# Cross-attention kernel: the layer norm of x moved from TensorE's transposes to a transposed load, a subtraction in place and a scale on the scores

## The chip, the cores and the metric

The kernel runs on one core of a Trainium2 chip. The metric is device time in microseconds (us) of one execution; a lower time is better. Five units work side by side and wait for each other through semaphores: TensorE (PE, matrix products and transposes), VectorE (DVE), ScalarE (ACT), GpSimd (POOL), and SyncE (SP), which here only issues transfers (DMAs). ACT issues a few DMAs too, on a queue of its own.

## The reference

x is (8, 128, 512), ctx is (8, 128, 512); there are 8 groups of 4 heads with 128 numbers each (H = 32 query heads, 8 key/value heads).

```
xn = layernorm(x)                       # (x - mean) / sqrt(var + 1e-5), over the 512
q, k, v = xn @ Wq, ctx @ Wk, ctx @ Wv   # Wq 512x4096, Wk and Wv 512x1024
q, k = rope(q), rope(k)                 # cos and sin rows gathered by position
scores = q k^T / sqrt(128), masked; attn = softmax(scores)
x = x + (attn v) @ Wo
x = x + ffn(layernorm(x))               # router, softmax, top 8, mix of 64 rows
```

The mean and the variance of a row of x are the same for all 512 columns of that row, and so (xn @ Wq) is ((x - mean) @ Wq) / sqrt(var + eps).

## The kernel before, in words

All matrix products run in two-part precision: each f32 operand is split into a rounded part (`hi`, by ACT) and a rest (`lo`, by DVE or POOL), and a product is three matmuls. The queries use Strassen's scheme with seven products (`m1` to `m7`) on half-size blocks. For that x is needed transposed (columns on partitions), as four blocks B11, B21, B12, B22 and four sums of them, T1 to T4; all lie in `x_raw`, and each is split into `x_hi` and `x_lo`.

The order of the work is written out by hand, engine by engine. The start of the program, up to about 125 us of the profiled execution, is the part that the change touches:

- SP issues the loads of ctx, Wv, x, Wk, the mask and the first query weights (`load_pair`), and between them the stores of the values (`store_v`, 16 pieces). SP's DMAs are served in the order of issue.
- PE computes 16 pieces of the values (lines 1824 to 1832 and 1847 to 1864), each into one of four PSUM banks; a bank is free again when DVE (pieces 0 to 9) or ACT (10 to 15, `copy_values`) has copied it to `v_stage`. A slot of `v_stage` is free when its store has landed (`dma_vout`). Between the pieces PE turns the gathered cos and sin rows (line 1810), and, after pieces 8 to 11, the normalised x (`transpose_x`, line 1844): 8 rows of the batch, four transposes of 128x128 each.
- DVE takes the statistics of x (lines 1318 to 1324), POOL raises var + eps to the power -0.5 (line 605), DVE normalises each batch row (`normalise_x`, line 1293), PE turns it, ACT copies it to `x_raw` (`copy_x`, line 918).
- POOL then builds the sums of the first query weights (`sums12`, `sum3`, `sum4`, line 554), two of their rests (`lo_w`, line 587), the x sums of the first batch half (`sum_x(0)`, lines 616 to 621), two more rests, and `sum_x(1)`. ACT rounds x (`hi_x`, line 928), DVE takes the rests (`lo_x`, line 1309), and between them both split Wk (`hi_wk` line 912, `lo_wk` line 1298). A third Wk tile can be loaded only when `lo_wk` has freed a slot of the two in `ring_a`.
- Then come 16 key products (lines 1866 to 1873, four banks again), each followed by a rotation: ACT swaps halves (lines 826, 827), POOL multiplies by sin (line 543), DVE by cos and adds (lines 1252, 1257). The first queries follow, and from about 140 us a loop over 64 steps (group, batch row) in which scores, softmax, values and output of one step overlap with the next group's queries. In each step DVE scales and masks the scores (line 1407, one instruction, the scale 128^-0.5 as a constant), ACT takes the exponentials (line 1005).

Of the kernel before, what the change touches and what calls it, by code (L numbers as in the profile page):

```python
# [18 lines left out]
F32 = mybir.dt.float32  # L19
# [45 lines left out]
X_AFTER = 8  # L65
X_ORDER = 0, 4, 1, 5, 2, 6, 3, 7
# [15 lines left out]
def xattn_ffn(nc, x, ctx, pos, mask, rope, wq, wk, wv, wo, router, router_bias, expert_bias, out):  # L82
    v_dram = nc.dram_tensor("v_dram", (KV * NH * P, HB * D), F32, kind="Internal").ap()
    k_dram = nc.dram_tensor("k_dram", (KV * P, T), F32, kind="Internal").ap()
    with ExitStack() as stack:
# [20 lines left out]
        kT = at("kT", [T], F32, 82)  # L106
        hold = at("hold", [5, W], F32, 86)
# [84 lines left out]
        x_rstd = at("x_rstd", [B], F32, 206.90625)  # L192
# [28 lines left out]
        x_bank = [probT, attnT]  # L221
# [28 lines left out]
        rstd_done = sem("rstd_done")  # L250
        norm_done = sem("norm_done")
# [6 lines left out]
        x_ps = sem("x_ps")  # L258
        x_copied = sem("x_copied")
# [137 lines left out]
        def _(sp):  # L397
# [35 lines left out]

            v_tiles = v_dram.rearrange("(g n p) (b d) -> n b p g d", g=KV, n=NH, d=D)
# [45 lines left out]
            sp.wait_ge(x_ps, B)  # L480
# [57 lines left out]
        def _(pool):  # L538
# [66 lines left out]
            pool.tensor_tensor(x_rstd[:, :], x_var[:, :], power[:, :], ALU.pow).then_inc(rstd_done, 1)  # L605
# [18 lines left out]
            pool.wait_ge(mask_done, 1)  # L624
            sum_x(0)
# [194 lines left out]
        def _(act):  # L820
# [93 lines left out]
            def copy_x(j):  # L914
                act.wait_ge(x_ps, j + 1)
                b = X_ORDER[j]
                half, rows = b // HB, slice(b % HB * S, (b % HB + 1) * S)
                act.activation(x_raw[:, 2 * half:2 * half + 2, :, rows],
                               x_bank[j % 2][:, :].rearrange("p (a c k) -> p a c k", a=2, c=HALVES), ACT.Copy).then_inc(x_copied, 1)

            def hi_x(i, q):

                cols = slice(q * 2 * S, (q + 1) * 2 * S)
                if i in (B11, B21, B22):
                    act.wait_ge(x_copied, (q + 1) * HB)
                else:
                    act.wait_ge(x_summed, 4 * (q + 1))
# [35 lines left out]
            copy_x(6)  # L963
            copy_x(7)
# [284 lines left out]
        def _(dve):  # L1249
# [62 lines left out]
            for i in range(V_ACT):  # L1312
                copy_values(i)
                if i in (3, 5):
                    half = 0 if i == 3 else 1
                    dve.wait_ge(dma_x[half], 16)
                    for b in range(half * HB, (half + 1) * HB):
                        dve.bn_stats(x_stats[:, b, :], resid[:, b, :]).then_inc(x_counted, 1)
                if i == 5:
                    dve.wait_ge(x_counted, B)  # L1320
                    for b in range(B):
                        dve.bn_aggr(x_mv[:, b, :], x_stats[:, b, :]).then_inc(x_averaged, 1)
                    dve.wait_ge(x_averaged, B)
                    dve.tensor_scalar(x_var[:, :], x_mv[:, :, 1], EPS, None, ALU.add).then_inc(var_done, 1)
# [3 lines left out]
                if i == X_AFTER - 1:  # L1328
                    dve.wait_ge(rstd_done, 1)
                    dve.wait_ge(b_lo, KB * C)  # L1330
                if i >= X_AFTER - 1:
                    normalise_x(2 * (i - X_AFTER + 1))
                    normalise_x(2 * (i - X_AFTER + 1) + 1)
            lo_wk(0)
            normalise_x(6)
            normalise_x(7)
# [109 lines left out]
            stored(0)  # L1446
            make_c11(0, 0)
# [295 lines left out]
        def _(pe):  # L1743
# [93 lines left out]
            def transpose_x(j):  # L1837
                pe.wait_ge(norm_done, j + 1)
                if j == 0:
                    pe.wait_ge(table_done, 2 * NH)  # L1840
                if j >= 2:
                    pe.wait_ge(x_copied, j - 1)
                for c in range(C):
                    last = pe.transpose(x_bank[j % 2][:, c * P:(c + 1) * P], x_norm[:, j % 2, c * P:(c + 1) * P], ident[:, :])
# [375 lines left out]
```

## Time and profile before

| what | value |
|---|---|
| time, median of 3 runs | 585.05 us (585.02 to 585.27) |
| the profiled execution: its time, its span | 585.23 us, 583.2 us |
| granted TensorE clock | 1.000 over the whole span |
| PE, DVE, ACT, POOL busy | 99%, 81%, 70%, 74% |
| chain that ended last, by engine | PE 92%, DVE 3%, issue 2%, ACT 2%, POOL 1% |
| DMA | 44.85 MB, mean 77 GB/s |

The span runs from the first to the last instruction. A busy share is a mean over stages with different limits: PE is busy nearly always, and the chain of waits (the work that ended last, followed backwards) runs through PE for 92% of the span. In the first 15 slices of 14.6 us the DMA engines are busy for most of the first two and little after. A granted clock of 1.000 means 2.4 GHz.

### The profile page before, as it was taken

What the parts mean: (1) busy time and instruction counts of PE and PEld (TensorE: products, weight loads), DVE (VectorE), ACT (ScalarE), POOL (GpSimd) and SP (SyncE); (2) the same over time, 40 slices, a digit from 0 to 9 for tenths busy, and PEclk for the clock granted to TensorE, in tenths of its full rate; (3) what the DMA queues carried; (4) which work ended last, traced back from release to release, by engine and by line L of the source; (5) the groups of instructions that cost most, each with busy time, mean ns of one, the idle gap of its engine ahead of it and who ended that gap; (6) DMA issues with size and microseconds to landing.
All of it is one profiled execution on the core that took longest, in us unless ns stands there. A gap on an engine that the chain in (4) does not pass through costs nothing.

```text
span 583.2 us, 10605 instructions
## 1 busy us (share of the span) xinstructions
PE 576.2 (99%) x2991; PEld 488.6 (84%) x2991; DVE 471.7 (81%) x764; ACT 406.3 (70%) x1078; POOL 430.8 (74%) x404
## 2 busy tenths in 40 slices
PE   9999999999999999999999999999999999999997
PEld 7788888877888888888888888888888888888885
DVE  5779797699797779877987798779877986797986
ACT  6377654797777767767776777777776776586655
POOL 5577699698986878688868886788678865446554
PEclk9999999999999999999999999999999999999999
DMA  8953526113301310131113110211122011100012
GB/s 278 367 166 97 169 90 216 38 37 103 97 19 56 91 55 20 54 90 54 32 40 90 54 54 20 88 54 54 36 72 69 3 57 54 36 20 0 19 38 90
DMA packets 30831, 44.85 MB, mean 77 GB/s; under 512 B 3024, under 2 KB 11600, under 8 KB 30800
## 3 DMA queue, kind: packets, MB, share of 16 engines
q1 hardware_dynamic: 30112, 43.56, 23.7%
q0 software_dynamic: 256, 0.52, 0.2%
q10 hardware_dynamic: 432, 0.40, 0.2%
q8 instruction: 14, 0.23, 0.2%
q14 instruction: 17, 0.14, 0.1%
HBM read 34.51 MB, written 9.96 MB: 76 GB/s over the span
## 4 chain that ended last, share of the span: by engine, by line
PE 92%; DVE 3%; issue 2%; ACT 2%; POOL 1%; DVEq 0%; ACTq 0%
PE score L1885 9%; PE outp L1909 9%; PE outp L1913 9%; PE outp L1917 8%; PE bank_a L1760 5%; PE bank_a L1762 5%; PE bank_a L1761 5%; PE probT L1964 4%; PE attnT L1746 2%; PE attnT L1747 2%; PE attnT L1748 2%; PE bank_c L1762 2%; PE bank_c L1760 2%; PE bank_c L1761 2%; PE bank_a L1746 1%
## 5 line engine op out<-in xcount | busy, mean ns | idle before, releaser
L543 POOL TENSOR_TENSOR rot<-rot,sinT 128x512 f32<-128x512 f32 x75 | 102.9, 1372 | 45.1 <-ACT rot L827 45.0
L1005 ACT ACTIVATE probs<-score,negmax 128x128 f32<-128x128 f32 x256 | 90.5, 366 | 28.6 <-DVE negmax L1415 28.6
L661 POOL TENSOR_TENSOR probs<-probs,rsum 128x512 f32<-128x512 f32 x62 | 67.1, 1083 | 44.2 <-DVE rsum L1421 44.2
L1909 PE MATMUL outp<-wo_hi,oT_hi 128*128 128x512 f32 x240 | 95.0, 398 | 0.2 <-DVE wo_lo L1482 0.2
L1913 PE MATMUL outp<-wo_lo,oT_hi 128*128 128x512 f32 x240 | 93.5, 391 | 0.3 <-POOL wo_lo L548 0.3
L1917 PE MATMUL outp<-wo_hi,oT_lo 128*128 128x512 f32 x240 | 83.4, 390 | 0.0
L1428 DVE TENSOR_TENSOR resid<-resid,outp 128x512 f32<-128x512 f32 x60 | 41.0, 684 | 48.8 <-PE outp L1917 46.9
L1885 PEld LDWEIGHTS score<-kT,qT 128*128 128x128 f32 x512 | 66.9, 191 | 4.9
L1257 DVE TENSOR_TENSOR qT<-qT,rot 128x512 f32<-128x512 f32 x57 | 68.5, 1205 | 2.9 <-POOL rot L543 0.5
L1132 ACT ACTIVATE oT_hi<-attnT 128x512 fp32r<-128x512 f32 x64 | 38.0, 594 | 43.1 <-PE attnT L1748 41.9
L1014 ACT ACTIVATE pT_hi<-probT 128x512 fp32r<-128x512 f32 x64 | 38.4, 599 | 42.5 <-PE probT L1964 41.9
L1885 PE MATMUL score<-kT,qT 128*128 128x128 f32 x512 | 67.4, 274 | 0.0
L1440 DVE TENSOR_TENSOR oT_lo<-attnT,oT_hi 128x512 fp32r<-128x512 f32 x64 | 44.2, 690 | 14.4 <-ACT oT_hi L1132 14.3
L548 POOL TENSOR_TENSOR wo_lo<-ring_b,wo_hi 128x512 fp32r<-128x512 f32 x30 | 38.6, 1318 | 21.6 <-ACT wo_hi L885 21.6
L1909 PEld LDWEIGHTS outp<-wo_hi,oT_hi 128*128 128x128 f32 x240 | 45.0, 188 | 10.3 <-DVE wo_lo L1482 1.1
L1917 PEld LDWEIGHTS outp<-wo_hi,oT_lo 128*128 128x128 f32 x240 | 45.1, 188 | 10.1
L1913 PEld LDWEIGHTS outp<-wo_lo,oT_hi 128*128 128x128 f32 x240 | 45.1, 188 | 9.9 <-POOL wo_lo L548 0.7
L1005 ACT ACTIVATION_READ_ACCUMULATOR probs<-score,negmax 128x1 f32 x256 | 52.0, 203 | 0.0
L1760 PE MATMUL bank_a<-x_hi,w_hi 128*128 128x512 f32 x120 | 51.9, 433 | 0.0
L1407 DVE SCALAR_TENSOR_TENSOR score<-score,mask_bias 128x512 f32<-128x512 f32 x64 | 44.5, 695 | 6.3 <-PE score L1885 3.0
L1762 PE MATMUL bank_a<-x_hi,w_lo 128*128 128x512 f32 x120 | 47.4, 395 | 0.0
L1761 PE MATMUL bank_a<-x_lo,w_hi 128*128 128x512 f32 x120 | 47.0, 391 | 0.0
(361 smaller groups left out, 1532.0 us busy)
## 6 DMA issues: line engine op xcount, KB each, us to landing
ring_b<-in_wo SPq DMA_DIRECT2D x32, 256.0 KB, 2.9
ring_a<-in_wq SPq DMA_DIRECT2D x28, 256.0 KB, 2.8
v_dram<-v_stage SPq DMA_DIRECT2D x16, 256.0 KB, 4.5
v_raw<-v_dram SPq DMA_DIRECT2D x16, 256.0 KB, 2.6
k_dram<-k_stage SPq DMA_DIRECT2D x14, 256.0 KB, 2.1
kT<-k_dram SPq DMA_DIRECT2D x14, 256.0 KB, 2.9
ctx_in<-in_ctx SPq DMA_DIRECT2D x8, 256.0 KB, 6.8
ring_b<-in_wv SPq DMA_DIRECT2D x8, 256.0 KB, 7.7
```

Of the source, the lines that this page charges most:

```text
L543: pool.tensor_tensor(rot_of(k0), rot_of(k0), sinT[:, half * W:(half + 1) * W], ALU.mult).then_inc(sin_done, 1)
L661: pool.tensor_tensor(probs[:, p], probs[:, p], rsum[:, p, :].unsqueeze(2).broadcast_to([P, GH, S]), ALU.mult).then_inc(soft_done, 1)
L1005: last = act.activation(probs[:, p, h, :], heads(score[p][:, :])[:, h, :], ACT.Exp, bias=negmax[:, p, h:h + 1], accum_out=sums[:, p, h:h + 1])
L1257: dve.tensor_tensor(dst, src, rot_of(k), ALU.add).then_inc(rope_done, 1)
L1407: dve.scalar_tensor_tensor(heads(score[p][:, :]), heads(score[p][:, :]), SCALE, mask_bias[:, b, :].unsqueeze(1).broadcast_to([P, GH, S]), ...
L1760: pe.matmul(ps[:, :], w[0], m[0], start=start and c == 0, stop=False, skip_group_check=True)
L1761: pe.matmul(ps[:, :], w[0], m[1], start=False, stop=False, skip_group_check=True)
L1762: last = pe.matmul(ps[:, :], w[1], m[0], start=False, stop=stop and c == HALVES - 1, skip_group_check=True)
L1885: last = pe.matmul(score[p][:, h * S:(h + 1) * S], qT[:, half, h, b % HB * S:(b % HB + 1) * S], kT[:, b * S:(b + 1) * S], start=True, stop ...
L1909: pe.matmul(ps[:, :], oT_hi[:, cols], wo_hi[:, h, :], start=h == 0, stop=False)
L1913: return pe.matmul(ps[:, :], oT_hi[:, cols], wo_lo[:, h, :], start=False, stop=stop)
L1917: return pe.matmul(ps[:, :], oT_lo[:, cols], wo_hi[:, h, :], start=False, stop=stop)
```

## The change

x is also handed over transposed (`xt`, 512 x 1024) and loaded from there straight into the four blocks of `x_raw`. The means, which DVE still computes from the untransposed x, are turned by PE (4 columns become 4 rows), copied out of PSUM by ACT, written to DRAM and read back as a broadcast to all 128 partitions, both on ACT's DMA queue; DVE then subtracts them from `x_raw` in place. 1/sqrt(var + eps) is no longer multiplied into x: POOL computes 1/sqrt(128 (var + eps)) per row, and this takes the place of the constant in the instruction that scales and masks the scores. `normalise_x`, `transpose_x` and `copy_x` are gone, with 8 of each. The order in the early part of the queues changes with it.

```diff
+            def load_xt(half):
+                cols = slice(half * W, (half + 1) * W)
+                for a in range(2):
+                    sp.dma_start(x_raw[:, 2 * half + a, :, :],
+                                 xt[a * HE:(a + 1) * HE, cols].rearrange("(c p) k -> p c k", p=P)).then_inc(dma_xt[half], 16)
...
             load_x(1)
-            for r in range(RA):
-                load_wk(r)
             sp.dma_start(mask_in[:, :, :], mask).then_inc(dma_mask, 16)
+            load_xt(0)
...
-            pool.tensor_tensor(x_rstd[:, :], x_var[:, :], power[:, :], ALU.pow).then_inc(rstd_done, 1)
+            pool.tensor_tensor(score_scale[:, :], x_var[:, :], power[:, :], ALU.pow).then_inc(scale_done, 1)
...
-                pool.wait_ge(x_copied, (q + 1) * HB)
+                pool.wait_ge(x_centred, NH + 1 + q)
...
+            def spread_mean(half):
+
+                act.wait_ge(mean_ps, half + 1)
+                act.activation(mean_row[:, half, :], mean_bank[half][0:HB, 0:S], ACT.Copy).then_inc(mean_copied, 1)
+                rows = mean_dram[half * HB:(half + 1) * HB, :]
+                act.wait_ge(mean_copied, half + 1)
+                act.dma_start(rows, mean_row[:, half, :]).then_inc(dma_mout[half], 16)
+                act.wait_ge(dma_mout[half], 16)
+                act.dma_start(x_mean[:, half * HB:(half + 1) * HB, :],
+                              rows.unsqueeze(0).broadcast_to([P, HB, S])).then_inc(dma_mean[half], 16)
...
             for half in range(NH):
                 copy_table(half)
+                spread_mean(half)
...
+            def centre_x(q, half):
+
+                if q == 0:
+                    dve.wait_ge(dma_xt[half], 32)
+                    dve.wait_ge(dma_mean[half], 16)
+                rows = slice(q * 2 * S, (q + 1) * 2 * S)
+                block = x_raw[:, 2 * half:2 * half + 2, :, rows].rearrange("p a c k -> p (a c) k")
...
+                dve.tensor_tensor(block, block, mean, ALU.subtract).then_inc(x_centred, 1)
...
-                    dve.tensor_scalar(x_var[:, :], x_mv[:, :, 1], EPS, None, ALU.add).then_inc(var_done, 1)
+                    dve.tensor_scalar(x_var[:, :], x_mv[:, :, 1], EPS, float(D), ALU.add, ALU.mult).then_inc(var_done, 1)
...
-                dve.scalar_tensor_tensor(heads(score[p][:, :]), heads(score[p][:, :]), SCALE,
+                dve.scalar_tensor_tensor(heads(score[p][:, :]), heads(score[p][:, :]), score_scale[:, b:b + 1],
...
+            def turn_mean(half):
+                pe.wait_ge(x_averaged, (half + 1) * HB)
+                pe.transpose(mean_bank[half][0:HB, 0:S], x_mv[:, half * HB:(half + 1) * HB, 0], ident[:, :]).then_inc(mean_ps, 1)
...
                 if i in TABLE_AFTER:
                     transpose_table(TABLE_AFTER.index(i))
-                if X_AFTER <= i < X_AFTER + HB:
-                    transpose_x(2 * (i - X_AFTER))
-                    transpose_x(2 * (i - X_AFTER) + 1)
+                    turn_mean(TABLE_AFTER.index(i))
```

Three queues show what moved. SP before, from the second load of x on: `early_pair_61` is the first query weight pair that is used, `early_pair_60` the second; `v_dram` rows are the stores of the values.

```order
L432 DMA resid<-in_x 128x4x512
L406 DMA ring_a<-in_wk 128x512 x2
L468 DMA mask_in<-in_mask 128x1024
L439 DMA v_dram<-v_stage 128x4x128 x3
L417 DMA early_pair_61<-in_wq 128x512 x2
L439 DMA v_dram<-v_stage 128x4x128 x4
L417 DMA early_pair_60<-in_wq 128x512 x2
```

SP now, from the same place (line numbers and buffer numbers are shifted; `early_pair_62` is the first pair that is used):

```order
L432 DMA resid<-in_x 128x4x512
L472 DMA mask_in<-in_mask 128x1024
L437 DMA x_raw<-in_xt 128x2x512 x2
L445 DMA v_dram<-v_stage 128x4x128 x2
L437 DMA x_raw<-in_xt 128x2x512 x2
L445 DMA v_dram<-v_stage 128x4x128
L417 DMA early_pair_62<-in_wq 128x512 x2
L445 DMA v_dram<-v_stage 128x4x128 x2
L406 DMA ring_a<-in_wk 128x512 x2
L445 DMA v_dram<-v_stage 128x4x128 x2
L417 DMA early_pair_61<-in_wq 128x512 x2
```

The four loads of xt (512 KiB each) stand ahead of the first query weights, the two loads of Wk (256 KiB each) behind them.

ACT before, from the table copies on, and then ACT now:

```order
L895 ACTIVATE cosT<-score 64x512 x2
L897 ACTIVATE sinT<-score 64x512
L898 ACTIVATE sinT<-score 64x512
L918 ACTIVATE x_raw<-probT 128x4x128
L918 ACTIVATE x_raw<-attnT 128x4x128
L912 ACTIVATE wk_hi<-ring_a 128x512 x2
L882 ACTIVATE w_hi<-early_pair_61 128x512
L882 ACTIVATE w_hi<-early_pair_61 128x256
```

```order
L905 ACTIVATE cosT<-score 64x512 x2
L907 ACTIVATE sinT<-score 64x512
L908 ACTIVATE sinT<-score 64x512
L927 ACTIVATE mean_row<-attnT 4x128
L930 DMA mean_dram<-mean_row 4x128
L932 DMA x_mean<-mean_dram 128x512
L892 ACTIVATE w_hi<-early_pair_62 128x512
L892 ACTIVATE w_hi<-early_pair_62 128x256
L922 ACTIVATE wk_hi<-ring_a 128x512 x2
L942 ACTIVATE x_hi<-x_raw 128x2x256 x3
```

Shown is the second half of the means; the first half stands the same way behind the first table copy, ahead of the second. Between the two DMAs ACT waits until the first has landed.

DVE before, from the copy of value piece 6 on (`outp` here), and then DVE now from the same copy:

```order
L1286 COPY v_stage<-outp 128x512
L1327 TENSOR_SCALAR mask_bias<-mask_in 128x1024
L1286 COPY v_stage<-bank_c 128x512
L1293 TENSOR_SCALAR x_norm<-resid,x_mv,x_rstd 128x512 x2
L1286 COPY v_stage<-bank_a 128x512
L1293 TENSOR_SCALAR x_norm<-resid,x_mv,x_rstd 128x512 x2
L1286 COPY v_stage<-bank_b 128x512
L1293 TENSOR_SCALAR x_norm<-resid,x_mv,x_rstd 128x512 x2
L1298 TENSOR_TENSOR wk_lo<-ring_a,wk_hi 128x512
L1293 TENSOR_SCALAR x_norm<-resid,x_mv,x_rstd 128x512 x2
```

```order
L1293 COPY v_stage<-outp 128x512
L1336 TENSOR_SCALAR mask_bias<-mask_in 128x1024
L1293 COPY v_stage<-bank_c 128x512
L1303 TENSOR_TENSOR x_raw<-x_raw,x_mean 128x4x256 x2
L1293 COPY v_stage<-bank_a 128x512
L1303 TENSOR_TENSOR x_raw<-x_raw,x_mean 128x4x256
L1293 COPY v_stage<-bank_b 128x512
L1303 TENSOR_TENSOR x_raw<-x_raw,x_mean 128x4x256
L1307 TENSOR_TENSOR wk_lo<-ring_a,wk_hi 128x512 x2
L1318 TENSOR_TENSOR x_lo<-x_raw,x_hi 128x2x256 x3
```

The copies of value pieces 8 and 9 (`bank_a`, `bank_b`) stand behind the subtractions, which wait for the first and the second half of the means. The first batch half of x is whole after the third subtraction.

## Rows read from the trace of the kernel before

**Rows 1.** The page: busy us; bandwidth in 40 slices of 14.6 us.
```profile
PE 576.2 (99%) x2991; PEld 488.6 (84%) x2991; DVE 471.7 (81%) x764; ACT 406.3 (70%) x1078; POOL 430.8 (74%) x404
...
GB/s 278 367 166 97 169 90 216 38 37 103 97 19 56 91 55 20 54 90 54 32 40 90 54 54 20 88 54 54 36 72 69 3 57 54 36 20 0 19 38 90
```
**Rows 2.** A stretch of 10 us: busy of PE, PEld, DVE, ACT, POOL; clock; DMA.
```profile
70.00:80.00 10.00, 10.00 (x46) 8.28 (x45) 9.41 (x10) 5.67 (x11) 10.00 (x8) 1.00 0.22 80
```
**Rows 3.** Chain of waits, 36 to 37 us: start, length, what.
```profile
36.17 0.44 PE probT L1844 x4
36.60 0.44 PE attnT L1844 x4
```
**Rows 4.** Timeline, POOL: start, length, instruction, [idle before it <- what ended it].
```profile
31.19 0.74 POOL L554 TENSOR_TENSOR w_sum<-early_pair 128x256 f32<-128x256 f32 x1 [1.47 <-DMA early_pair<-in_wq]
...
35.78 2.17 POOL L587 TENSOR_TENSOR w_lo<-early_pair,w_hi 128x512 fp32r<-128x512 f32 x2 [1.47 <-ACT w_hi L882]
37.91 1.47 POOL L616 TENSOR_TENSOR x_raw<-x_raw 128x512 f32<-128x512 f32 x1
...
42.59 1.35 POOL L621 TENSOR_TENSOR x_raw<-x_raw 128x512 f32<-128x512 f32 x1
...
98.20 3.12 POOL L543 TENSOR_TENSOR rot<-rot,sinT 128x512 f32<-128x512 f32 x2
```
**Rows 5.** Timeline, ACT.
```profile
23.85 1.19 ACT L895 ACTIVATE cosT<-score 64x512 f32<-64x512 f32 x2 [2.40 <-PE score L1810]
...
25.68 0.59 ACT L898 ACTIVATE sinT<-score 64x512 f32<-64x512 f32 x1
...
54.18 2.20 ACT L928 ACTIVATE x_hi<-x_raw 128x512 fp32r<-128x512 f32 x4 [3.04 <-POOL x_raw L621]
...
59.43 0.64 ACT L912 ACTIVATE wk_hi<-ring_a 128x512 fp32r<-128x512 f32 x1 [2.05 <-DMA ring_a<-in_wk]
59.96 0.58 ACT L945 ACTIVATE v_stage<-bank_c 128x512 f32<-128x512 f32 x1
...
113.72 0.60 ACT L826 ACTIVATE rot<-bank_a 64x512 f32<-64x512 f32 x1 [0.59 <-PE bank_a L1762]
...
125.25 0.60 ACT L862 ACTIVATE part_u<-bank_a 128x512 f32<-128x512 f32 x1 [0.41 <-PE bank_a L1762]
```
**Rows 6.** Timeline, DVE.
```profile
44.41 5.19 DVE L1309 TENSOR_TENSOR x_lo<-x_raw,x_hi 128x512 fp32r<-128x512 f32 x3
...
55.82 0.68 DVE L1298 TENSOR_TENSOR wk_lo<-ring_a,wk_hi 128x512 fp32r<-128x512 f32 x1
...
100.66 1.81 DVE L1257 TENSOR_TENSOR k_stage<-k_stage,rot 128x512 f32<-128x512 f32 x2
...
104.20 0.69 DVE L1389 TENSOR_TENSOR hold<-probT,part_s 128x512 f32<-128x512 f32 x1 [1.12 <-PE probT L1762]
```
**Rows 7.** Timeline, PE: first matmul of value piece 13 and of key product 3.
```profile
46.88 0.39 PE L1746 MATMUL bank_b<-wv_hi,ctxT_hi 128*128 128x512 f32 x1
...
63.20 0.39 PE L1746 MATMUL bank_c<-ctxT_hi,wk_hi 128*128 128x512 f32 x1
```
**Rows 8.** DMAs: tiles, queue, operation, count, KB of one, us from issue to landing.
```profile
table<-in_rope,pos_idx POOLq DMA_INDIRECT x8, 6.2
...
out<-ff_end ACTq DMA_DIRECT2D x1, 128.0 KB, 2.4
rbias<-in_router_bias SPq DMA_DIRECT2D x1, 32.0 KB, 5.3
pos_in<-in_pos ACTq DMA_DIRECT2D x1, 4.0 KB, 2.9
```
**Rows 9.** Groups of DVE: count, busy us, mean ns, idle before them.
```profile
L1407 DVE SCALAR_TENSOR_TENSOR score<-score,mask_bias 128x512 f32<-128x512 f32 x64 | 44.5, 695 | 6.3 <-PE score L1885 3.0
...
L1428 DVE TENSOR_TENSOR resid<-resid,outp 128x512 f32<-128x512 f32 x60 | 41.0, 684 | 48.8 <-PE outp L1917 46.9 <-PE outp L1913 1.9
...
L1647 DVE SCALAR_TENSOR_TENSOR ff_out<-bank_b,ff_rsum,ff_y 128x512 f32<-128x512 f32 x4 | 3.0, 751 | 2.1 <-PE bank_b L2067 2.1
```

More of the change, by code:

```diff
@@ L79, with xattn_ffn @@
 KEEP = 4, 1
-def xattn_ffn(nc, x, ctx, pos, mask, rope, wq, wk, wv, wo, router, router_bias, expert_bias, out):
+def xattn_ffn(nc, x, xt, ctx, pos, mask, rope, wq, wk, wv, wo, router, router_bias, expert_bias, out):
     v_dram = nc.dram_tensor("v_dram", (KV * NH * P, HB * D), F32, kind="Internal").ap()
     k_dram = nc.dram_tensor("k_dram", (KV * P, T), F32, kind="Internal").ap()
+    mean_dram = nc.dram_tensor("mean_dram", (B, S), F32, kind="Internal").ap()
     with ExitStack() as stack:
@@ L249, in xattn_ffn @@
         var_done = sem("var_done")
-        rstd_done = sem("rstd_done")
-        norm_done = sem("norm_done")
+        scale_done = sem("scale_done")
+        dma_xt = [sem(f"dma_xt{i}") for i in range(NH)]
+        mean_ps = sem("mean_ps")
+        x_centred = sem("x_centred")
+        mean_copied = sem("mean_copied")
+        dma_mout = [sem(f"dma_mout{i}") for i in range(NH)]
+        dma_mean = [sem(f"dma_mean{i}") for i in range(NH)]
         mask_done = sem("mask_done")
@@ L465, in _ @@
             load_x(1)
-            for r in range(RA):
-                load_wk(r)
             sp.dma_start(mask_in[:, :, :], mask).then_inc(dma_mask, 16)
+            load_xt(0)
             for i in range(KB * B):
                 store_v(i)
+                if i == 1:
+                    load_xt(1)
                 if i == 2:
                     load_pair(1, 0)
+                if i == 4:
+                    for r in range(RA):
+                        load_wk(r)
                 if i == 6:
@@ L1318, in _ @@
                         dve.bn_stats(x_stats[:, b, :], resid[:, b, :]).then_inc(x_counted, 1)
+                    dve.wait_ge(x_counted, (half + 1) * HB)
+                    for b in range(half * HB, (half + 1) * HB):
+                        dve.bn_aggr(x_mv[:, b, :], x_stats[:, b, :]).then_inc(x_averaged, 1)
                 if i == 5:
-                    dve.wait_ge(x_counted, B)
-                    for b in range(B):
-                        dve.bn_aggr(x_mv[:, b, :], x_stats[:, b, :]).then_inc(x_averaged, 1)
                     dve.wait_ge(x_averaged, B)
-                    dve.tensor_scalar(x_var[:, :], x_mv[:, :, 1], EPS, None, ALU.add).then_inc(var_done, 1)
+                    dve.tensor_scalar(x_var[:, :], x_mv[:, :, 1], EPS, float(D), ALU.add, ALU.mult).then_inc(var_done, 1)
                 if i == 6:
@@ L1327, in _ @@
                     dve.tensor_scalar(mask_bias[:, :, :], mask_in[:, :, :], 0.0, MASKED, ALU.is_equal, ALU.mult).then_inc(mask_done, 1)
[L1328 to L1333, printed above, removed]
+                if i == 7:
+                    centre_x(0, 0)
+                    centre_x(1, 0)
+                if i == 8:
+                    centre_x(0, 1)
+            centre_x(1, 1)
             lo_wk(0)
[L1335 to L1336 removed]
             lo_wk(1)
@@ L1835, in _ @@
                         last.then_inc(proj_done, 1)
[L1837 to L1844, printed above, removed]
-                last.then_inc(x_ps, 1)
+            def turn_mean(half):
+                pe.wait_ge(x_averaged, (half + 1) * HB)
+                pe.transpose(mean_bank[half][0:HB, 0:S], x_mv[:, half * HB:(half + 1) * HB, 0], ident[:, :]).then_inc(mean_ps, 1)
             for i in range(len(early_banks), KB * B):
```

45 lines of the change are left out of this document (12 added, 33 removed).

## The prediction

> **What bounds the kernel now.** I read the page first, then the stretches of the first 150 us, then the timelines of the engines there, and the DMAs last. The page says that PE is busy for 99% of the span [rows 1]; the reader is to see in it that a matmul less is a gain only as long as nothing else becomes late. The bandwidth line says something about the start alone: in its second slice (14.6 to 29.2 us) the DMA engines move 367 GB/s, four times the average of later slices [rows 1]. The stretches show a second full engine behind PE: POOL is busy for all of 70 to 80 us [rows 2], and the last two key rotations still start the moment POOL is free, at 98.20, and end at 101.32 [rows 4]. So the key phase has two bounds side by side, PE and POOL, and POOL's work is started by a chain that begins with x: sums of x on POOL, rests of x on DVE, which free the Wk slots, which ACT waits for before it copies value piece 15 and begins the first rotation [rows 4 to 6]. PE runs some us ahead of that chain: the copy of piece 15 ends at 60.54 [rows 5], and PE takes its bank at 63.20 [rows 7], a margin of 2.7 us.
>
> **The change part by part.** All sums are made against the profiled execution: 585.23 us, of which 583.2 are its span and 2.0 lie around it; the median of the runs is 0.2 lower.
>
> PE. Gone are 8 groups of four transposes at 0.44 us each [rows 3], 3.5 us; new are two single transposes, a quarter of such a group each, 0.2 us. PE is full there, so this alone is -3.3 us, 581.9 us, if no wait takes its place.
>
> DMA. SP's transfers are served in their order of issue, and up to about 34 us there is always one waiting. Ahead of the first query weights stand now 2 MiB of xt more and 0.5 MiB of Wk less: 1.5 MiB, 1.57 MB, at 367 GB/s 4.3 us; the broadcast of the first half of the means (256 KiB, on ACT's queue, but on the same engines) is another 0.7. POOL waited for these weights until 31.19 [rows 4]; now until 36.2. Bounds: 0 (if the engines had room) and 5.0. I take 5.0, because the second slice shows no room [rows 1]. The Trainium skill says the same against this change (DMA: Bandwidth & Descriptors, "Issuing engines are not separate DMA queues"): transfers issued by several engines share the same 16 DMA engines, so that ACT's queue buys no bandwidth; a run of this trace with two busy queues at full load is not to be seen.
>
> POOL's part of the x chain. From the weights' landing POOL needs 3.1 us of sums (31.19 to 34.31, when its wait of 1.47 before 35.78 begins) and 2.2 us of rests [rows 4] before the x sums. Before, ACT's late rounding cost 1.5 us between them; that goes. So the x sums can start at 36.2 + 3.1 + 2.2 = 41.5, against 37.91 before [rows 4].
>
> The means. ACT ends the first table copy at 26.27 (23.85 to 25.68 + 0.59) [rows 5]; the small copy I estimate at 0.4, so the store is issued at 26.7. The trace has no small store under load. From below there is ACT's store at the idle end, 2.4 us, from above the gathers of the loaded start, 6.2; I take 2.9, the load that ACT itself issued in the first us while SP's loads ran [rows 8]. The broadcast has one relative, the router bias, 5.3 us [rows 8], which I take, with 2.4 and 6.2 as its bounds as well. ACT stands still until the store has landed, at 29.6; behind it wait the second table copy (2.4), the second copy of means (0.4) and the first weights' rounding. With 0.4 for an issue: 30.0 + 2.8 + 2.9 + 5.3 = 41.0 for the second half on all partitions. DVE then subtracts 1024 columns: two inputs from SBUF, so twice 0.68 us with POOL idle and twice 1.73 (5.19 / 3) with POOL at work [rows 6]. I take 1.4; both halves of x are there at 42.4, bounds 38.5 (2.4 for each DMA) and 52.0 (6.2 for each, subtraction 3.5). The x sums start at the later of 41.5 and 42.4. Value copies 8 and 9 stand behind these waits on DVE: copy 9 is done at 43.1, and PE wants its bank for piece 13 at 46.88 - 3.3 = 43.6 [rows 7], which just holds.
>
> On the subtraction the Trainium skill (SBUF — State Buffer, "SBUF: two separate sides") has a rule against it: a DVE operation with two SBUF inputs and a GpSimd operation that reads SBUF lock each other out of one port pair for a whole instruction. The trace agrees: 1.73 against 0.68 us, above. By it the third subtraction, beside POOL's rests, would take 3.5, and the sum below would end 2.1 higher. Another page speaks for the change (DMA: Bandwidth & Descriptors, "Anatomy of one DMA — SWDGE (gpsimd) path"): about 2.0 us fixed and the bytes over 436 GB/s for a transfer; an estimate from it is 36.5 for the second half of the means instead of 41.0, POOL's 41.5 would decide, and the sum below would be 0.9 lower.
>
> What is late next. The x sums are 42.4 - 37.9 = 4.5 us later than before. The next waits in the chain take some of it back: DVE began the rests 0.47 after POOL's sums were done (43.94, 44.41) [rows 4, 6], leaving 4.0. ACT's copy of piece 15, behind the Wk tile that it waited 2.05 us for, ends at 64.5 instead of 60.54 [rows 5]. PE, 3.3 us earlier, wants the bank at 59.9 and gets it at 64.6: the whole 3.3 is waited away, between pieces 14 and key product 3, and 1.4 more. POOL's rotations, back to back, are 4.0 later; the last addition of the keys ends at 106.5 instead of 102.47 [rows 6]. From there the first queries pass from DVE to ACT to POOL and back, one by one, and three waits for PE shrink: 0.4 (a part of the 1.12 before 104.20, since the swap that follows is held up by the sum ahead of it) [rows 6], 0.59 at 113.72 and 0.41 at 125.25 [rows 5]. Left are 4.0 - 1.4 = +2.6 us, and the steps after 140 us, led by PE, carry that to the end.
>
> The scale. 64 instructions read their scale per partition instead of a constant. The same operation with such a scalar, an f32 tensor and an SBUF output takes 751 ns, the present one 695 [rows 9]: at most 3.6 us of DVE. DVE waits 48.8 us for PE in front of the additions of the same steps [rows 9], so I cost it at nothing; without that cover it is those 3.6, and a gain has no source. At nothing as well: POOL's power (same instruction), DVE's eight normalisations of 0.5 to 1.5 us and ACT's eight copies of 0.6, because neither engine was the last in its chain there; they make the room in which the means are spread.
>
> **The sum:** 585.2 + 2.6 = 587.8, and 587.6 on the scale of the median.
>
> **The rivals.** With the start of the x sums at s, the end moves by (s - 37.9) - 1.9.
> *Faster: the cover holds.* The xt loads find room, the weights land within 1.5 us of before, the means at their lower bound: s = 38 gives -1.8, 583.4; the floor is PE's own -3.3, 581.9. For it: the DMA bandwidth falls to 166 GB/s in the third slice [rows 1], so 1.5 MiB do fit before 44 us. Against it: SP's order puts them ahead of the weights, not behind. It takes s under 38.7. Chance 0.14.
> *No change: gain and delay meet.* s = 41.5 (means early) gives +1.7, and POOL and DVE, no longer in step, block each other 1 to 2 us less in the stretch of 65 to 101 us, where rest operations take 0.68 or 1.73 [rows 6]: 585.0 to 586. Against it: POOL's list of work there is the same. Chance 0.23.
> *Slower by far: the means' way through DRAM.* Four transfers in a row, each near 6.2 under load: s = 52 gives +12.2, 597; half of that excess, s = 47, gives +7.2, 592. It decides from s = 45 on, when the second half lands after 43.6. Against it: 6.2 includes POOL's own work for a gather. Chance 0.11.
> *The forecast,* s of 41.5 to 45, +1.7 to +5.2 (587 to 590): chance 0.52.
>
> **How the numbers follow.** A measurement of this kernel tells about 0.2% (1.2 us) from no change. Faster by more than that: 0.14. Within it: 0.23. Slower: 0.52 + 0.11 = 0.63. The range of 583.0 to 592.0 leaves out the floor of the faster rival and the far half of the slow one, under 2 in 10; the forecast's own range is 586.8 to 590.2.
>
> **What would show it.** Right: POOL's first sums of weights released by their DMA near 36; the first x sum near 42, released by DVE's subtraction; PE idle some 4 to 5 us in all in front of value piece 15 and key products 2 and 3, waiting for ACT's copies; POOL without a gap up to about 105; then everything some 2 to 3 us behind the trace of before. Wrong: weights landing near 32; PE without waits between 40 and 65 us; the x sums before 39, or after 45; waits for DVE's mask operation in the 64 steps. A granted clock below 1.00 in the first 150 us would also take the ground from the sum, since all durations here are from rows at 1.00.

## The result, and the profile after

The changed kernel takes 591.02 us (median of 4 runs, 590.47 to 591.16) against 585.03: slower by 6.0 us, ratio 1.010 with a 95% interval of 1.0087 to 1.0112. The direction was as forecast, but +2.6 us was forecast and +6.0 came: the time lies within the stated range of 583.0 to 592.0, which was wide, and above the 586.8 to 590.2 of the forecast itself. The profiled execution took 591.16 us, its span 589.0, 5.8 more than before.

The page after, engines and bandwidth as in [rows 1]:

```profile
PE 576.2 (98%) x2961; PEld 485.9 (83%) x2961; DVE 474.2 (81%) x760; ACT 402.6 (68%) x1072; POOL 433.0 (74%) x404
...
GB/s 283 381 282 101 177 75 193 92 38 29 133 55 55 90 53 20 54 89 53 18 53 89 53 18 53 89 53 49 23 88 53 18 40 68 37 19 1 19 38 90
```

PE is busy as long as before although its work is 3.3 us shorter (a part of that is a stretch at a lower clock, shown with e4), and the third slice, 166 GB/s before, now carries 282. ACT's timeline after (start, length, instruction, idle before it and what ended it; ACTq is its queue for DMAs):

```profile
26.09 0.27 ACT L927 ACTIVATE mean_row<-probT 4x128 f32<-4x128 f32 x1
26.38 0.52 ACTq L930 DMA_DIRECT2D mean_dram<-mean_row  x1
30.50 0.35 ACTq L932 DMA_DIRECT2D x_mean<-mean_dram  x1
30.90 1.20 ACT L905 ACTIVATE cosT<-score 64x512 f32<-64x512 f32 x2 [4.54 <-DMA mean_dram<-mean_row]
...
33.64 0.27 ACTq L930 DMA_DIRECT2D mean_dram<-mean_row  x1
37.68 0.33 ACTq L932 DMA_DIRECT2D x_mean<-mean_dram  x1
...
65.46 0.64 ACT L922 ACTIVATE wk_hi<-ring_a 128x512 fp32r<-128x512 f32 x1 [2.22 <-DMA ring_a<-in_wk]
66.00 0.58 ACT L960 ACTIVATE v_stage<-bank_c 128x512 f32<-128x512 f32 x1
```

Each store of 2 KB of means holds ACT for 4.0 to 4.1 us, from 26.38 to 30.50 and from 33.64 to 37.68. The last two rows answer to those at 59.43 and 59.96 in [rows 5]: the Wk tile and the copy of piece 15 come 6.0 us later.

POOL's timeline after, and then DVE's:

```profile
33.86 0.75 POOL L563 TENSOR_TENSOR w_sum<-early_pair 128x256 f32<-128x256 f32 x1 [5.14 <-DMA early_pair<-in_wq]
...
36.07 1.74 POOL L563 TENSOR_TENSOR w_sum<-early_pair,w_sum 128x256 f32<-128x256 f32 x1
38.83 2.00 POOL L596 TENSOR_TENSOR w_lo<-early_pair,w_hi 128x512 fp32r<-128x512 f32 x2 [1.01 <-ACT w_hi L892]
43.41 1.30 POOL L625 TENSOR_TENSOR x_raw<-x_raw 128x512 f32<-128x512 f32 x1 [2.59 <-DVE x_raw L1303]
44.79 2.15 POOL L627 TENSOR_TENSOR x_raw<-x_raw 128x512 f32<-128x512 f32 x1
46.91 1.74 POOL L628 TENSOR_TENSOR x_raw<-x_raw 128x512 f32<-128x512 f32 x1
48.72 1.60 POOL L630 TENSOR_TENSOR x_raw<-x_raw 128x512 f32<-128x512 f32 x1
```

```profile
42.02 1.23 DVE L1303 TENSOR_TENSOR x_raw<-x_raw,x_mean 128x1024 f32<-128x1024 f32 x1 [2.53 <-DMA x_mean<-mean_dram]
...
43.76 2.03 DVE L1303 TENSOR_TENSOR x_raw<-x_raw,x_mean 128x1024 f32<-128x1024 f32 x1
45.71 3.48 DVE L1307 TENSOR_TENSOR wk_lo<-ring_a,wk_hi 128x512 fp32r<-128x512 f32 x2
50.36 5.12 DVE L1318 TENSOR_TENSOR x_lo<-x_raw,x_hi 128x512 fp32r<-128x512 f32 x3 [1.17 <-POOL x_raw L630]
...
61.69 0.68 DVE L1307 TENSOR_TENSOR wk_lo<-ring_a,wk_hi 128x512 fp32r<-128x512 f32 x1
```

The weights land at 33.86 (31.19 in [rows 4]). The x sums start at 43.41 instead of 37.91, released by DVE's subtraction, and the first four take until 50.3, 6.9 us instead of 6.0; beside them DVE runs its fourth subtraction and two rests of Wk, where before it ran the two rests and two normalisations. DVE's first rest of x starts at 50.36 instead of 44.41 [rows 6].

PE's waits after, from 15 to 130 us (us in total, times, longest); before there was none over 0.2 us from 20 to 130:

```profile
PE bank_c L1754 <- ACT v_stage L960: 3.7, 2, 3.4
PE outp L1768 <- ACT part_u L872: 0.7, 1, 0.7
PE bank_a L1768 <- ACT part_t L866: 0.5, 1, 0.5
PE bank_b L1754 <- DVE v_stage L1293: 0.5, 1, 0.5
...
```

The longest stands in front of value piece 15 (its bank waits for ACT's copy of piece 11, done at 53.0), within the stretch that was forecast. PE begins the first query product at 102.16 instead of 98.56, the first scores come 5.4 us later than before.

ACT among the first queries, the same three places as 113.72, 115.38 and 125.25 before (the first and the last are in [rows 5], with waits of 0.59 and 0.41 for PE; the second had no wait):

```profile
118.70 0.60 ACT L836 ACTIVATE rot<-bank_a 64x512 f32<-64x512 f32 x1
...
120.75 0.60 ACT L836 ACTIVATE rot<-outp 64x512 f32<-64x512 f32 x1 [0.40 <-DVE qT L1264]
...
130.63 0.60 ACT L872 ACTIVATE part_u<-bank_a 128x512 f32<-128x512 f32 x1 [0.41 <-PE bank_a L1770]
```

The first of the two waits for PE is gone, but a wait of 0.40 for DVE's `qT` stands behind it; the other is as long as before.

### The profile page after: what moved, and what is told of

The parts are those of the page before. It is cut to its first block, busy times and chain, and to the rows that moved or that the text cites. A ratio compares the mean times of both kernels' runs of the same rounds, so it can differ in the third digit from the quotient of the medians.

```text
span 589.0 us, 10537 instructions
## 1 busy us (share of the span) xinstructions
PE 576.2 (98%) x2961; PEld 485.9 (83%) x2961; DVE 474.2 (81%) x760; ACT 402.6 (68%) x1072; POOL 433.0 (74%) x404
## 4 chain that ended last, share of the span: by engine, by line
PE 72%; DVE 5%; POOL 5%; issue 4%; ACT 3%; DMA 1%; SPq 0%; DVEq 0%; POOLq 0%; ACTq 0%
PE score L1885 9%; PE outp L1909 8%; PE outp L1913 8%; PE outp L1917 8%; PE bank_a L1768 4%; PE bank_a L1770 4%; PE probT L1964 4%; PE bank_a L1769 4%; PE attnT L1754 2%; PE attnT L1755 2%; PE attnT L1756 2%; PE bank_c L1768 2%; PE bank_c L1769 2%; PE bank_c L1770 2%; POOL rot L552 2%
## 5 line engine op out<-in xcount | busy, mean ns | idle before, releaser
L552 POOL TENSOR_TENSOR rot<-rot,sinT 128x512 f32<-128x512 f32 x75 | 103.0, 1374 | 44.5 <-ACT rot L837 44.2
L1021 ACT ACTIVATE pT_hi<-probT 128x512 fp32r<-128x512 f32 x64 | 38.4, 599 | 41.5 <-PE probT L1964 41.0
L1447 DVE TENSOR_TENSOR oT_lo<-attnT,oT_hi 128x512 fp32r<-128x512 f32 x64 | 44.1, 689 | 14.5 <-ACT oT_hi L1139 14.1
L1414 DVE SCALAR_TENSOR_TENSOR score<-score,score_scale,mask_bias 128x512 f32<-128x512 f32 x64 | 48.3, 755 | 5.9 <-PE score L1885 2.4
```

Of the source, the lines that this page charges most:

```text
L552: pool.tensor_tensor(rot_of(k0), rot_of(k0), sinT[:, half * W:(half + 1) * W], ALU.mult).then_inc(sin_done, 1)
```

## The experiments

Theory at the start: the means' way through DRAM decides when the x sums begin, the weights, with which POOL is done 2.6 us before the first x sum starts, would decide next, and what PE saved is waited away. Code cuts are shortened; `...` marks what is left out. Times are medians; "before" was run beside each and lay at 584.8 to 585.1.

**The scale alone (e1).**

```diff
-  tensor_scalar(x_norm, resid, x_mv[..0:1], x_rstd, subtract, mult)
+  tensor_scalar(x_norm, resid, x_mv[..0:1], 1.0, subtract, mult)
...
-  tensor_scalar(x_var, x_mv[..1], EPS, None, add)
+  tensor_scalar(x_var, x_mv[..1], EPS, float(D), add, mult)
...
-  scalar_tensor_tensor(score, score, SCALE, mask_bias, ...)
+  scalar_tensor_tensor(score, score, x_rstd[:, b:b + 1], mask_bias, ...)
```

> The kernel before with one part of the change alone: 1/sqrt(var) goes into the scale of the scores, per row, and x is still normalised (mean only) by VectorE and turned by TensorE. Theory (the 5.9 us were lost in the first 70 us, on the way of x): the 64 scale-and-mask instructions grow from 695 to about 755 ns, 3.8 us of VectorE, all hidden behind its waits for TensorE; 585.0 us, within 0.6 of before. Rival (the longer instruction stands in every step's chain): 3 to 4 us more, 588 to 589, with TensorE waiting for VectorE in the steps.

585.32 us, ratio 1.0006 (0.9997 to 1.0015): as the theory had it. DVE's group of 64, to be read beside [rows 9]:

```profile
L1407 DVE SCALAR_TENSOR_TENSOR score<-score,x_rstd,mask_bias 128x512 f32<-128x512 f32 x64 | 48.3, 755 | 6.3 <-PE score L1885 3.0
```

60 ns more each, 3.8 us of DVE in all, and PE waits for none of it.

**Without the means' way (e2).**

```diff
+  pool.memset(x_mean, 0.0)    # early on POOL; subtracted in place of the means
...
   copy_table(half)            # on ACT
-  spread_mean(half)
```

> The changed kernel with the spreading of the means left out: ScalarE neither copies, stores nor reloads them, and VectorE subtracts a tile of zeros, so x stays with its means; all else is as in the changed kernel. Theory (the way of the means through DRAM decides when the x sums start): the x sums start when POOL has done the weights, at 39.8 instead of 43.4 us (weights landing at 33.9, 3.95 of sums, 2.0 of rests, no wait for ScalarE), and no subtraction runs beside them (6.0 instead of 6.9 us): 4.5 us less, 586.5. Rival (the load of 2 MiB of transposed x and the weights' delay behind it decide): 590 to 591, no change, as the weights still land near 34.

587.12 us, ratio 1.0037 (1.0023 to 1.005): 3.9 us of the 6.0 are the means' way. The first four x sums start 2.4 us earlier than in the changed kernel and take 5.3 us instead of 6.9, with nothing of DVE beside them. They start at 41.05, not 39.8, since a subtraction and two rests of Wk, now earlier, ran beside POOL's weight work. POOL and then DVE in this kernel:

```profile
33.87 1.18 POOL L564 TENSOR_TENSOR w_sum<-early_pair 128x256 f32<-128x256 f32 x1 [5.19 <-DMA early_pair<-in_wq]
...
36.53 1.72 POOL L564 TENSOR_TENSOR w_sum<-early_pair,w_sum 128x256 f32<-128x256 f32 x1
38.20 2.90 POOL L597 TENSOR_TENSOR w_lo<-early_pair,w_hi 128x512 fp32r<-128x512 f32 x2
```

```profile
35.84 1.81 DVE L1304 TENSOR_TENSOR x_raw<-x_raw,x_mean 128x1024 f32<-128x1024 f32 x1
37.57 2.93 DVE L1308 TENSOR_TENSOR wk_lo<-ring_a,wk_hi 128x512 fp32r<-128x512 f32 x2
```

**First weights ahead of xt (e3).**

```diff
+  load_pair(1, 0)
   load_xt(0)
...
-  if i == 2:
-      load_pair(1, 0)
```

> The changed kernel with the first query weight pair loaded ahead of all of the transposed x instead of behind three quarters of it. Theory (means' way): the weights land near 29 instead of 33.9, but the x sums still wait for the second half of the means at 42.0 and start at 43.4; 591.0, within 0.6. Rival (the weights' delay decides): the x sums start some 3 us earlier, 588.

590.88 us, ratio 1.0104 (1.0089 to 1.012): no change, as expected. POOL begins with the weights at 28.45, without a wait, then stands 6.74 us for ACT's rounding, which is behind the second store of means, and the x sums start at 42.99.

**PE's work given back (e4).**

```diff
+  if B <= i < B + HB:
+      for c in range(2 * C):
+          pe.transpose(early_bank(u)[:, ...], ident, ident)
```

> The changed kernel with as much TensorE work put back as the change took out: 32 single transposes of the identity ahead of value pieces 8 to 11 (eight each, 3.5 us), in banks that the piece then overwrites; nothing waits for them. Theory (what TensorE saves is waited away in front of value piece 14, whose bank ScalarE frees late): 591.0 to 591.5, and that wait of 3.4 us shrinks to near nothing. Rival (TensorE's own work sets the end): 594.5.

591.03 us, ratio 1.0102 (1.0086 to 1.0117), as expected: 3.5 us of PE more cost nothing. The wait of 3.4 (it stands before piece 15, not 14 as the expectation counts) falls to 0.2; one of 1.9 now stands later, before key product 2. This run also shows what the clock is worth here. PE's stretches (busy, clock, DMA) of the changed kernel, and then of this one:

```profile
54.00:56.00 2.00, 2.00 (x7) 0.57 0.43 128
56.00:58.00 2.00, 2.00 (x7) 0.57 0.05 12
```

```profile
54.00:56.00 2.00, 2.00 (x11) 1.00 0.43 128
56.00:58.00 2.00, 2.00 (x11) 1.00 0.01 4
```

After its wait of 3.4 us the changed kernel's PE is granted mostly 1.2 GHz for these 4 us (0.57 is a mean of the two levels); here it keeps 2.4 GHz, and the time is the same, with a wait of 1.9 still to spare.

**Means spread by PE (e5).**

```diff
   copy_table(half)
-  spread_mean(half)
...
-  pe.transpose(mean_bank[half][0:HB, 0:S], x_mv[:, half rows, 0], ident)
+  for b in range(HB):
+      pe.transpose(mean_bank[half][:, b * S:(b + 1) * S], x_mv[:, b, 0:1].broadcast_to([P, S]), ident)
...
-  mean = x_mean[...]           # SBUF, through DRAM
+  mean = mean_bank[half][...]  # PSUM
```

> The changed kernel with the means spread by TensorE instead of through DRAM: eight transposes of a mean column repeated 128 times put the means of all rows on all partitions in PSUM, and VectorE subtracts from there. Theory (two late inputs: the means' way, then the weights' load): without the DRAM way the weights (33.9) decide, as in the run without the means, x sums from 40 to 41; TensorE's extra 0.7 us are hidden; and because VectorE now reads one input from PSUM, POOL's weight sums beside it take 0.74 us and not 1.2 to 1.7. 586 to 587. Rival (the subtraction itself costs the time, whatever its source): 590 to 591.

585.65 us, ratio 1.0014 (1.0005 to 1.0023), a little better than expected. POOL and DVE:

```profile
33.50 0.74 POOL L563 TENSOR_TENSOR w_sum<-early_pair 128x256 f32<-128x256 f32 x1 [4.83 <-DMA early_pair<-in_wq]
...
38.83 1.74 POOL L625 TENSOR_TENSOR x_raw<-x_raw 128x512 f32<-128x512 f32 x1
```

```profile
36.44 1.21 DVE L1302 TENSOR_TENSOR x_raw<-x_raw,attnT 128x1024 f32<-128x1024 f32 x1
```

With one input in PSUM the subtraction takes 1.21 us beside a busy POOL (1.81 in e2), and POOL's weight sums take 0.74 (1.18 and 1.72 there). The Trainium skill (SBUF — State Buffer, "Who interferes with whom") states it so: a VectorE instruction with at most one input in SBUF, outside the modes that use two ports, doesn't contend with GpSimd. These rows agree.

**Both late inputs mended (e8)**: e5 and e3 together.

> Both late inputs mended: the means spread by TensorE through PSUM, and the first weight pair loaded ahead of the transposed x. Theory: weights at 28.4, x whole and centred by 35 to 36, x sums from about 36.5, earlier than before the change (37.9); nothing waits, and TensorE's saving shows: 3.5 us of transposes less, 0.9 of new ones, so 582.4, at most 583.2. Rival (some other part of the change, the per-row scale or the moved Wk loads, costs time that the late inputs hid): 585 or more.

583.05 us, ratio 0.9971 (0.9959 to 0.9982): faster than before the change. POOL:

```profile
28.64 0.73 POOL L562 TENSOR_TENSOR w_sum<-early_pair 128x256 f32<-128x256 f32 x1
...
33.08 2.00 POOL L595 TENSOR_TENSOR w_lo<-early_pair,w_hi 128x512 fp32r<-128x512 f32 x2 [1.07 <-ACT w_hi L891]
36.17 1.30 POOL L624 TENSOR_TENSOR x_raw<-x_raw 128x512 f32<-128x512 f32 x1 [1.09 <-DVE x_raw L1301]
```

Means late and weights late 591.0, only means late 590.9 (e3), only weights late 585.65, neither 583.05: the later input decides, and the other is worth something only when the first is gone.

**Two sums into POOL's gap (e6).**

```diff
+  sums12(0, 0)          # ahead of the rotations
   for k, (g, half) in enumerate(KEYS):
...
-      if k == 1:
-          sums12(0, 0)
```

> The changed kernel with the first two sums of the second weight pair moved ahead of the key rotations on POOL, into the 8 us that it idles there (60.2 to 67.9); the rest as it was. Theory (from 70 to 107 us POOL's rotations, back to back and 6.0 us late, hold the first queries; TensorE itself is only 3.6 us late at its first query product): POOL ends the rotations 2.3 us earlier, then TensorE's 3.6 us and POOL's 3.65 are level: 589.0 to 589.7. Rival (TensorE's waits before 66 us set the end alone): 591.0, no change.

590.77 us, ratio 1.0104 (1.0089 to 1.012): a miss. POOL ended the rotations 0.5 us earlier, not 2.3: the two sums ran beside DVE's rests of x, the sixth Wk tile came 0.84 later (ACT's rounding at 66.30), and in the rotations other operations of POOL took longer. POOL's head start was lost again, and so the run does not decide between the theory and its rival.

**Wk rests into DVE's wait (e9).**

```diff
   if i == 8:
+      lo_wk(0)
+      lo_wk(1)
       centre_x(0, 1)
   centre_x(1, 1)
-  lo_wk(0)
-  lo_wk(1)
```

> The changed kernel with VectorE's rests of the first two Wk tiles moved ahead of the third subtraction, into its wait for the second half of the means, so that they no longer run beside POOL's first x sums. Theory (two operations with both inputs in SBUF slow each other: the four x sums took 6.9 us beside them, 5.2 with VectorE idle): the x sums take some 0.7 to 0.9 us less, and copy 15, the rotations and the end come as much earlier: 590.2 to 590.5. Rival (the lengthening of the x sums is hidden): 591.0.

590.58 us, ratio 1.0103 (1.0088 to 1.0119): 0.44 below the changed kernel, too little for the intervals; the verdict is the trace's. The x sums take 6.1 us instead of 6.9 (43.57 to 49.69), and copy 15 comes 0.75 earlier:

```profile
47.05 1.28 POOL L628 TENSOR_TENSOR x_raw<-x_raw 128x512 f32<-128x512 f32 x1
48.41 1.28 POOL L630 TENSOR_TENSOR x_raw<-x_raw 128x512 f32<-128x512 f32 x1
```

By then I held that every us by which the second x sums end later costs one at the end. Four runs tried that.

**Rests behind the x sums (e10), the same in e8 (e11), and the same before the change (e12).**

```diff
   sum_x(0)
-  lo_w(W1, 1, 0)
-  lo_w(W2, 1, 0)
   sum_x(1)
+  lo_w(W1, 1, 0)
+  lo_w(W2, 1, 0)
```

> The changed kernel with two of POOL's weight rests (3.0 us) moved from between the two halves of the x sums to behind them, where POOL idles 8 us. Theory (over the seven kernels run so far the time is the end of the second x sums plus 531.1, within 0.3: every us of the x chain costs one): the x sums end 3.0 us earlier, near 57.0, and the time is 588.0 to 588.3. Rival (the prediction's reckoning, in which the next waits absorb up to 1.9 us, or POOL's total of work counts): 589.5 to 591.

591.03 us, ratio 1.0099 (1.0084 to 1.0115): the theory falls. The second x sums end 3.4 us earlier, and the sixth Wk tile and copy 15 don't move. POOL, DVE and ACT:

```profile
50.30 1.27 POOL L625 TENSOR_TENSOR x_raw<-x_raw 128x512 f32<-128x512 f32 x1
...
56.60 3.44 POOL L596 TENSOR_TENSOR w_lo<-w_sum,w_hi 128x512 fp32r<-128x512 f32 x2
```

```profile
50.38 5.12 DVE L1318 TENSOR_TENSOR x_lo<-x_raw,x_hi 128x512 fp32r<-128x512 f32 x3 [1.17 <-POOL x_raw L630]
...
61.72 0.68 DVE L1307 TENSOR_TENSOR wk_lo<-ring_a,wk_hi 128x512 fp32r<-128x512 f32 x1
```

```profile
65.38 0.63 ACT L922 ACTIVATE wk_hi<-ring_a 128x512 fp32r<-128x512 f32 x1 [4.26 <-DMA ring_a<-in_wk]
```

So it is the end of the first four x sums, at which DVE starts its rests, and not that of the second four.

> The kernel with both late inputs mended (means by TensorE through PSUM, first weights ahead of the transposed x), with the same two rests behind the x sums. Theory: the x sums end near 49; now TensorE's own work is the floor, 585.0 less 3.5 plus 0.9: 582.4, so 0.3 to 0.7 better than 583.05 and no more. Rival (the x chain is still the only bound): 580 to 580.3.

583.25 us, ratio 0.9972 (0.9961 to 0.9983): the rival falls, and the 0.3 to 0.7 that the theory still saw did not come either. The time is that of e8, 0.9 above the floor that was expected; what holds it there is not shown.

> The kernel before with the same two rests moved behind the x sums and nothing else. Theory (in the kernel before TensorE and the x chain bind side by side; TensorE never waited between 20 and 125 us): the x sums end 3 us earlier and nothing is gained: 584.7 to 585.2. Rival (the x chain alone binds it too): 582.

585.10 us, ratio 1.0001 (0.9992 to 1.001): no change, as expected, though after e10 it no longer tells the two apart.

**The x chain delayed before the change (e13).**

```diff
+  for half in range(NH):
+      pool.tensor_tensor(kT[:, half], resid[:, half], resid[:, half], add)
   sum_x(0)
```

> The kernel before with two additions of 128x512 put on POOL ahead of the first x sums, into a tile that is not yet in use: a delay of 2.6 to 3.1 us for the x chain, with TensorE's work as it was. Theory (no slack in the chain): 587.5 to 588.2. Rival (the prediction's reckoning: 1.9 us are absorbed on the way to the queries): 585.7 to 586.3.

586.47 us, ratio 1.0023 (1.0013 to 1.0034): between the two. POOL's additions took 2.67 us, but the weights landed 1.1 earlier in this run, so that the first x sums ended 2.35 later than before and DVE's rests began 1.92 later, at 46.33; 1.4 reached the end. Some slack there is, 1.0 us, about half of the 1.9 that the prediction took.

All kernels so far in one table: start of DVE's first rest of x, start of its first masking of scores, and the time.

| kernel | first x rest | first scores masked | apart | time |
|---|---|---|---|---|
| e11, e8 | 42.0, 42.3 | 118.6, 118.6 | 76.6, 76.3 | 583.25, 583.05 |
| before, e12, e1 | 44.4, 44.5, 44.1 | 121.4, 121.5, 121.0 | 77.0 each | 585.0, 585.1, 585.3 |
| e5 | 44.6 | 121.0 | 76.4 | 585.65 |
| e13, e2 | 46.3, 46.4 | 122.7, 122.7 | 76.4, 76.3 | 586.5, 587.1 |
| e9, e3, e6 | 49.7, 49.9, 50.3 | 126.1, 126.2, 126.4 | 76.4, 76.3, 76.1 | 590.6, 590.9, 590.8 |
| e4, after, e10 | 50.4 each | 126.7, 126.8, 126.7 | 76.3 to 76.4 | 591.0 each |

76.3 us lead from DVE's first rest of x to the scores, over 8 us of difference; only the kernels with the old PE work and no delay, and e11, stand above it; I take it that PE sets the pace there. Three more runs asked what those 76.3 us begin with.

**Order and amount of DVE's rests (f1, f3, f2).** f1 changes the order, f3 puts two rests of x behind the first rotations, f2 does both.

```diff
-  for i in range(3):
+  for i in range(2):
       lo_x(i, 0)
   lo_wk(2)
-  for i in range(3, 7):
-      lo_x(i, 0)
+  lo_x(2, 0)
   lo_wk(3)
+  for i in range(3, 7):
+      lo_x(i, 0)
```

> The changed kernel with VectorE's rests of the third and fourth Wk tile moved ahead of three and four of the x rests, so that the two slots of Wk come free earlier; the same work in another order. Theory W (from the end of the first x sums a chain of fixed length leads on: x rests on VectorE, rest of the fourth Wk tile, its slot, the load of the sixth tile, ScalarE's rounding, copy 15): that rest ends near 57.8 instead of 62.4, copy 15 near 63.9 instead of 66.6; VectorE's own work still ends at 66.8, so the rotations and the end gain 1.1 to 2: 589 to 590. Rival V (VectorE's amount of work from 50.4 to 66.8 is what holds the keys, not its order): 591.0.

588.68 us, ratio 1.0071 (1.0057 to 1.0085): 2.3 us less from the order alone. Copy 15 ends at 63.9 as theory W had it, 2.7 us earlier than in the changed kernel, and the first scores come 2.6 earlier. DVE and ACT:

```profile
56.73 1.78 DVE L1307 TENSOR_TENSOR wk_lo<-ring_a,wk_hi 128x512 fp32r<-128x512 f32 x1
58.44 5.39 DVE L1318 TENSOR_TENSOR x_lo<-x_raw,x_hi 128x512 fp32r<-128x512 f32 x7
```

```profile
62.80 0.62 ACT L922 ACTIVATE wk_hi<-ring_a 128x512 fp32r<-128x512 f32 x1
63.32 0.58 ACT L960 ACTIVATE v_stage<-bank_c 128x512 f32<-128x512 f32 x1
```

The edit of f3:

```diff
-  for i in range(3, 5):
-      lo_x(i, 1)
   lo_wk(5)
...
-  if k in (2, 3):
-      lo_x(k + 3, 1)
+  if k in (2, 3, 4, 6):
+      lo_x({2: 3, 3: 4, 4: 5, 6: 6}[k], 1)
```

> The changed kernel with two more x rests (1.3 us) moved behind the first key rotations on VectorE, the Wk rests where they were. Theory W: the slot of the fourth Wk tile comes free as before, at 62.4, and copy 15 ends at 66.6: 591.0, no change. Rival V: VectorE is free 1.3 us earlier, and the time is 589.7.

591.81 us, ratio 1.0118 (1.0103 to 1.0133): less work for DVE ahead of the rotations gains nothing. The first rotation starts 0.6 us earlier than in the changed kernel, but the scores come 0.4 later: the two rests cost something behind the rotations, where PE waits 0.9 for a copy of ACT.

f2 has the edits of f1 and f3.

> Both edits together: the Wk rests earlier and two more x rests behind the first rotations. Theory W: copy 15 ends near 63.9 and VectorE is free near 65.5, so the rotations start some 2.5 us earlier: 588.3 to 589. Rival V: 589.7, the same as with the second edit alone.

589.45 us, ratio 1.0073 (1.0059 to 1.0087): a miss for the forecast of theory W (588.3 to 589), no better than f1 alone, and by its time alone near rival V's 589.7. The trace shows why: copy 15 ends at 64.1 and the first rotation starts 2.4 us earlier, as W has it, but the scores come only 0.9 earlier; the two rests put behind the first rotations cost the difference, as in f3. Rival V falls on f1 (588.68 where it had 591.0) and f3 (591.81 where it had 589.7). So up to the rotations theory W holds: rests of x, rest of the fourth Wk tile, its slot, a load of 3 us, ACT's rounding, copy 15. The chain of waits in the changed kernel runs the same way (start, length, what), where before it lay on PE alone from 36 to 125 us:

```profile
61.76 0.61 DVE wk_lo L1307
...
62.39 2.98 DMA ring_a<-in_wk
...
66.00 0.58 ACT v_stage L960
...
70.16 1.26 POOL rot_key L552
```

## Why the prediction was right in sign and wrong in size

The mechanism was forecast rightly: the means' way through DRAM decides when the x sums start, and what PE saves is waited away. The start, s = 43.41, lies within the 41.5 to 45 that the forecast allowed. The step that failed is the next one, from s to the end, "(s - 37.9) - 1.9": for 43.4 it gives +3.6, and the span grew by 5.8. Term by term:

- **PE, -3.3 us if no wait takes its place.** Right, and a wait took its place (e4). Where the inputs come in time, 1.8 us net can be had (e8, 583.05 against 584.84 of the kernel before beside it).
- **Weights at 36.2.** Too late: 33.86, 2.7 us behind before instead of 5.0. The prediction took the DMA engines as full at 367 GB/s. From 14.6 us to the weights' landing they moved 361 GB/s before and 379 now, from the program's start to there 322 and 338: there was some room. (367 is nearly six times the average of the later slices, not four.) This error was made good by another: from the landing POOL needed 7.0 us, not 5.3, since its last sum took 1.74 beside DVE's first subtractions and it still waited 1.0 for ACT's rounding, which the second store held back. It was ready at 40.8 (41.5 forecast), too early to decide.
- **Means at 41.0, x sums at 42.4.** 42.02 and 43.41, 1.0 later. The stores held ACT for 4.1 and 4.0 us where I took 2.9 each; the second broadcast landed 4.3 after its issue where I took 5.3. The second estimate for the same time, 36.5, was off by 5.5. The subtraction of 1.4 came true, with POOL idle beside it.
- **Length of the x sums.** Put at no change; 6.9 us instead of 6.0, so +0.9. With DVE idle beside them they take 5.3 (e2); before, two rests of Wk and two normalisations stood beside them, now the two rests and a subtraction with both inputs in SBUF, which I did not count against POOL. With the rests moved away they take 6.1 (e9).
- **"The next waits in the chain take some of it back", 1.9 us.** 1.0 us was taken back. Of the 6.4 us by which the first x sums ended later, 0.4 went before DVE's rests (0.47 forecast) and 0.55 before the first scores (1.4 forecast): DVE's rests began 5.95 later, copy 15 ended 6.04 later, the scores 5.4. I had counted three waits for PE as room. The one of DVE is gone and gave 0.5 (0.4 forecast). The 0.59 of ACT is gone too, but then ACT waits 0.40 for DVE, which is as late as the rest. The 0.41 of ACT stands as before, because PE, which waits 0.55 and 0.70 for ACT's copies before it, has become as late as the chain there. e13 measures the slack by itself, with PE's work as before: 1.0.
- **The scale at nothing.** Nearly: e1 shows +0.3 (-0.2 to +0.9). In the changed kernel 0.4 us more lie between the first and the last masking (431.35 instead of 430.91), in e2 and e5 as well (431.27 each), in e1 only 0.1; so the scale alone is not all of it, and what else it is stays open.

The sum with the measured terms: 5.5 for the start of the x sums, 0.9 for their length, -0.4 and -0.55 of slack, 0.4 behind the first scores: 5.8, the difference of the spans. So of the 3.2 us that the forecast fell short, 1.0 is the means' way, 0.9 the length of the x sums, 0.9 the slack and 0.4 what lies behind the first scores. None alone would have put the forecast right. The rival of a slow way through DRAM has the same mechanism as the forecast; it was to decide from s = 45 on, and s was 43.4. Of the signs of being wrong one came, a granted clock below 1.00; it did not matter (e4).

## What to carry to other kernels

Follow a chain past the wait that you remove or add down to the place where it meets the bounding engine again, and count slack only where an engine is idle for another reason than the one that you delay. Work that an edit makes later lands beside something: look up what, and whether both read two tensors from SBUF. Statistics that all partitions need can be spread by a transpose of a repeated column into PSUM, without DRAM; here that alone is worth 5.4 us, and with the weights loaded first the change becomes a gain of 0.3%.

## What was not expected of the hardware

A store of 2 KB to DRAM, issued by ACT while the DMA engines moved 372 to 388 GB/s, held the next step for 4.0 to 4.1 us; the 128 KB store at the idle end of the program takes 2.4 [rows 8]. A broadcast of 256 KB took 4.3 to 5.5. The masking with a scale per partition takes 755 ns, the one with a constant 695 [rows 9]. The fall of PE's clock to about half over 4 us cost nothing here (e4); I take it that PE was ahead of the chain that it waits for next.
